# One woven section for the last two attention layers of a four-layer kernel

## The reference

```python
# second layer here ("L2"): 16 heads, 16 wide
a = layer_norm(ctx) ; Q = x @ Wq.T ; K = a @ Wk.T ; V = a @ Wv.T
scores = where(mask, Q K' / 4, -inf) ; out = softmax(scores) V @ Wo.T
x = x + tanh(gate) * out
# third layer here ("L3"): 32 query heads, 8 key heads, 8 wide
q = x @ Wq + bq ; k = ctx @ Wk + bk ; v = ctx @ Wv + bv
scores = q k' / sqrt(8) + mask ; out = softmax(scores) v @ Wo + bo
x = layer_norm(out + x) * gamma + beta
```

## Time and profile before

| | |
|---|---|
| median of 3 runs | 1299.11 us (1297.94 to 1301.02) |
| profiled execution, its own time | 1306.43 us |
| its span, first to last instruction | 1304.7 us |
| the last two layers in it | from 946.1 us to the end |
| TensorE busy over the span | 1163.8 us (89%) |
| VectorE, ScalarE, GpSimd busy | 852.4, 638.6, 655.9 us |

### The profile page before, as it was taken

One profiled execution on the slowest core, in us unless ns is written; L12 is line 12 of the kernel. 1 busy time (PEld: TensorE's weight loads), 2 busy tenths in 40 slices (PEclk: granted clock), 3 DMA queues, 4 the chain that ended last, 5 costly groups with the idle time before them and its releaser, 6 DMA issues. The chain is left out here.

```text
span 1304.7 us, 20610 instructions
## 1 busy us (share of the span) xinstructions
PE 1163.8 (89%) x7388; PEld 903.4 (69%) x7388; DVE 852.4 (65%) x2097; ACT 638.6 (49%) x1428; POOL 655.9 (50%) x677
## 2 busy tenths in 40 slices
PE   6999999999999999999999769986768998899994
PEld 4788888888888888888788624433436765666664
DVE  6776665766756766667756555985545657666756
ACT  3655655556655565455662114203133672477770
POOL 3665665556646565466763032770022661277760
PEclk9999999999999999999999869998888999899997
DMA  6210121112210112012102000000020000000000
GB/s 205 66 49 17 66 65 49 48 35 65 66 49 21 62 65 66 23 43 65 65 18 80 17 0 1 1 0 1 0 90 1 2 2 1 1 1 2 2 2 33
DMA packets 35110, 47.05 MB, mean 36 GB/s; under 512 B 3865, under 2 KB 22082, under 8 KB 35010
## 3 DMA queue, kind: packets, MB, share of 16 engines
q1 hardware_dynamic: 34640, 44.83, 10.7%
q10 hardware_dynamic: 370, 0.91, 0.2%
HBM read 44.69 MB, written 1.05 MB: 35 GB/s over the span
## 5 line engine op out<-in xcount | busy, mean ns | idle before, releaser
L444 POOL TENSOR_TENSOR a_prob<-a_prob,a_inv_total 128x512 f32<-128x512 f32 x128 | 144.3, 1127 | 208.3 <-DVE a_inv_total L732 208.3
L1583 POOL TENSOR_TENSOR l_scores<-l_scores,l_neg_max 128x512 f32<-128x512 f32 x144 | 147.8, 1041 | 103.1 <-DVE l_neg_max L1573 102.8
L1573 DVE CUSTOM_DVE_ANT_0 l_scores<-psum,mask 128x256 f32<-128x256 f32 x384 | 139.8, 421 | 72.9 <-PE psum L1526 72.9
L637 ACT ACTIVATE a_prob<-psum,a_neg_max 128x257 f32<-128x257 f32 x256 | 119.2, 473 | 94.2 <-DVE a_neg_max L729 93.5
L1604 ACT ACTIVATE l_prob_T<-psum 128x512 f32<-128x512 f32 x192 | 108.8, 590 | 37.2 <-PE psum L1540 37.2
L1540 PE MATMUL psum<-ident,l_scores 128*128 128x128 f32 x768 | 117.8, 292 | 7.3 <-POOL l_scores L1583 4.3
L1540 PEld LDWEIGHTS psum<-ident,l_scores 128*128 128x128 f32 x768 | 86.3, 147 | 42.1 <-issue 19.8
L736 DVE TENSOR_TENSOR a_probT_lo<-psum,a_probT_hi 128x512 fp32r<-128x512 f32 x128 | 88.0, 688 | 32.7 <-ACT a_probT_hi L641 32.1
L566 PE MATMUL psum<-ident,a_prob 128*128 128x128 f32 x512 | 77.8, 274 | 24.1 <-DVE a_probT_lo L736 21.7
L566 PEld LDWEIGHTS psum<-ident,a_prob 128*128 128x128 f32 x512 | 60.0, 140 | 44.7 <-issue 21.2
L729 DVE TENSOR_REDUCE a_neg_max<-psum 128x2 f32<-128x514 f32 x128 | 87.3, 682 | 1.2 <-PE psum L486 1.2
(11 more groups left out here) (331 smaller groups left out, 3294.9 us busy)
## 6 DMA issues: line engine op xcount, KB each, us to landing
wk_raw<-in_L_xattn_wk SPq DMA_DIRECT2D x16, 512.0 KB, 6.4
wq_raw<-in_L_xattn_wq SPq DMA_DIRECT2D x16, 512.0 KB, 5.7
wv_raw<-in_L_xattn_wv SPq DMA_DIRECT2D x16, 512.0 KB, 3.9
wo_raw<-in_L_xattn_wo SPq DMA_DIRECT2D x16, 512.0 KB, 4.0
ctx_rows<-in_ctx SPq DMA_DIRECT2D x3, 512.0 KB, 4.6
x_rows<-in_x SPq DMA_DIRECT2D x2, 512.0 KB, 9.6
mask<-in_mask_Bx1xSxS_ff SPq DMA_DIRECT2D x1, 1024.0 KB, 9.0
out_dram<-fin_y SPq DMA_DIRECT2D x4, 256.0 KB, 2.1
```

Source lines behind the costliest of these rows:

```text
L444: pool.tensor_tensor(prob[:, m % 4, :, 0:S], prob[:, m % 4, :, 0:S], rtot[:, m % 4, :].unsqueeze(2).to_broadcast([P, 2, S]), ALU.mult)
L637: act.activation(prob[:, m % 4, q, 0:S + 1], s_bank(g)[:, q, 0:S + 1], ACT.Exp, bias=negm[:, m % 4, q:q + 1], accum_out=tot[:, m % 4, q:q ...
L1573: e = dve.tensor_tensor_reduce(sc[:, i % SC, q, :], s_bank(i)[:, q * S:(q + 1) * S], masks[:, b * NM + q % NM, :], 1.0, BIG, ALU.add, ALU. ...
L1583: pool.tensor_tensor(sc[:, i % SC, :, :], sc[:, i % SC, :, :], m[:, i % SC, :].unsqueeze(2).to_broadcast([P, 2, S]), ALU.subtract).then_in ...
```

## The change

The ten blocks become one. `last_layers_orders` writes one order per engine by hand: an opening, then all 192 heads in a row, then an ending. Everything else is cut into pieces, each of one bank: `XT2`, `CT`, `AT` (turns of `x`, context and normalised context), `Q`, `K`, `V` of one half of the sequences, `SQ`, `SK` (stacks), `OT`, `OB`, `OP` (turn and divide the sums, turn back, output product) of one sequence, and `XT3` (turn of the new `x`).

- The opening holds the first half's pieces of the second layer up to the stacks, in 8 banks. Then come the scores of heads 0 to 3, the first half's `V` and the second half's `AT`, and the heads.
- Behind head i's `turn`, TensorE does the piece `behind[i]`: one piece behind each of heads 0 to 25, 28 to 57 and 60 to 71, then one behind every second head from 73 to 95 and in 99 to 109, 131 to 141, 163 to 173, 179 and 181. All of them use bank 7, so a piece waits until the one before it is evicted. Sums have one bank (6) where they had two.
- VectorE takes the extremes up to head i + 2 before it evicts the piece behind head i. Projections are now read twice straight from their bank: ScalarE rounds (hi), then VectorE subtracts (lo).
- To GpSimd go: clearing and filling the selection matrices (40 small copies), scaling both query weights, negating the third layer's mask, ones and zeros beside the values, the third layer's output bias, and scale and offset of the final norm for sequences 0 to 2.
- Loads have a semaphore each. The third layer's mask lands in the context's rows once these are read.
- Moments and final norm are done sequence by sequence; only sequence 3's lie behind the last head.

The core of the diff:

```diff
-        with ExitStack() as st:
-            ln = LayerNorm(...)
-            run_layernorm(chip, ln, load, turns=((chip.x, xT), (chip.ctx, cT)), vector_then=make_mask, scalar_then=make_gate)
-        attend(L2, w2, xT, aT, (None, None, None), masks2, gated)
-        stage_turn_and_bias(chip, chip.x, xT, chip.rows[:, r:r + 1, :], mask3)
-        attend(L3, w3, xT, cT, (...), mask3, ...)
-        stage_final_norm(chip, out)
+    put(0, [('CT', 1, c) for c in range(NC)] + [('Q', 2, 1, c) for c in range(NC)] + [('K', 2, 1, c) for c in range(NC)]
+        + [('SQ', 2, 1, g) for g in range(4)] + [('SK', 2, 1, g) for g in range(8)] + [('V', 2, 1, n) for n in range(2)])
+    put(20, output_pieces(2, 0) + [('XT3', 0), ('K', 3, 0, 0)])
+    put(28, [('SK', 3, 0, g) for g in range(7)])
+    put(35, output_pieces(2, 1) + [('XT3', 1), ('SK', 3, 0, 7)] + [('Q', 3, 0, c) for c in range(NC)]
+        + [('SQ', 3, 0, g) for g in range(8)] + [('V', 3, 0, 0)])
...
+    put(163, output_pieces(3, 2), 2)
+    put(179, output_pieces(3, 3)[:2], 2)
+    ending = output_pieces(3, 3)[2:]
+    bank = {p: k % 8 for k, p in enumerate(opening)}
+    bank.update(zip(second, (7, 6, 4, 5)))
+    bank.update({p: F_BANK for p in behind.values()})
+    pe = [('F', p) for p in opening] + [('S', 0), ('S', 1)] + [('F', p) for p in second]
+    for i in range(HEADS):
+        pe.append(('T', i))
+        if i in behind:
+            pe.append(('F', behind[i]))
+        if i % 2 and i // 2 + 2 < HEADS // 2:
+            pe.append(('S', i // 2 + 2))
+        if i % 4 == 1 and i > 4:
+            pe.append(('A', i // 4 - 1))
...
+                def piece(p):
+                    kind, bank = p[0], ps[:, bank_of[p], :]
+                    if earlier[p]:
+                        landed(pe, [earlier[p]])
...
+                for i in range(HEADS):
+                    if not on_scalar(i):
+                        pool.wait_ge(s_read, i + 1)
+                        pool.tensor_tensor(sc[:, i % SC, :, :], sc[:, i % SC, :, :],
+                                           m[:, i % SC, :].unsqueeze(2).to_broadcast([P, 2, S]), ALU.subtract).then_inc(shifted, 1)
+                    extras(i)
+                inverse_deviation(B - 1)
```

More of the change, by code:

```diff
@@ L1305, in __init__ @@
         self.per_chunk = P // (4 * width)
-L2 = Small("l2", 16, 16, 16, 16 ** -0.5, 2)
-L3 = Small("l3", 32, 8, 8, 1.0 / float(np.sqrt(np.float32(8.0))), 1)
+        self.KC = max(1, self.kv_cols // P)
+        self.KR = min(P, self.kv_cols)
+SMALL = {2: Small(16, 16, 16, 16 ** -0.5, 2), 3: Small(32, 8, 8, 1.0 / float(np.sqrt(np.float32(8.0))), 1)}
 BIG = 3e38
-def stage_turn_and_bias(chip, rows, out, bias, mask):
-    nc, ps = chip.nc, chip.psum
[L1317 to L1337, removed]
@@ L1340, in stage_small_project @@
[L1340 to L1349, removed]
-    with ExitStack() as st:
[L1351 to L1358, removed]
-        with nc.Block() as block:
+N2, N3 = B * SMALL[2].H, B * SMALL[3].H
@@ L1379, in _ @@
[L1379 to L1388, removed]
@@ L1552, in sums @@
                                            pT[:, i % PT, t * S:(t + 1) * S], start=t == 0, stop=t == 1, tile_position=(0, 32 * j))
                     mm.then_inc(a_done, 1)
-                scores(0)
-                scores(1)
-                for i in range(N):
-                    turn(i)
-                    if i % 2 and i // 2 + 2 < N // 2:
-                        scores(i // 2 + 2)
-                    if i % 4 == 1 and i > 4:
-                        sums(i // 4 - 1)
-                sums(QUADS - 1)
@@ L1577, in _ @@
-            @block.gpsimd
-            def _(pool):
-                for i in range(N):
-                    if on_act(i):
-                        continue
-                    pool.wait_ge(s_read, i + 1)
-                    pool.tensor_tensor(sc[:, i % SC, :, :], sc[:, i % SC, :, :],
-                                       m[:, i % SC, :].unsqueeze(2).to_broadcast([P, 2, S]), ALU.subtract).then_inc(shifted, 1)
+                for kind, what in pe_order:
+                    if kind == 'F':
+                        if what == output_pieces(3, 3)[2]:
+                            pe.wait_ge(s_read, HEADS)
+                        piece(what)
+                    elif kind == 'S':
+                        scores(what)
+                    elif kind == 'T':
+                        turn(what)
+                    else:
+                        sums(what)
@@ L1597, in shift, with exp @@
                     e.then_inc(act_shifted, 1)
-                shift(2)
-                for i in range(N):
+                def exp(i):
                     act.wait_ge(turned, i + 1)
@@ new lines, in exp @@
+                    act.activation(pT[:, i % PT, :], t_bank(i), ACT.Exp, scale=1.0 if on_scalar(i) else -1.0).then_inc(exp_ok, 1)
+                for kind, what in act_order:
+                    if kind == 'E':
+                        evict(what)
+                    elif kind == 'exp':
+                        exp(what)
+                    elif kind == 'shift':
+                        shift(what)
+                    elif kind == 'keep':
+                        keep(what)
+                    else:
+                        act.wait_ge(ld['gate'], 16)
+                        act.activation(gate[:, :], gate[:, :], ACT.Tanh).then_inc(gate_ok, 1)
```

806 lines of the change are left out of this document (487 added, 319 removed).

## The result

The kernel after takes 1311.99 us (median of 4 runs, 1311.25 to 1314.12), the kernel before 1299.47 beside it (1297.94 to 1301.02). The ratio is 1.0099, 95% interval 1.0081 to 1.0116: slower. I had forecast 1278 and a range of 1256 to 1297.

The account below looks back on a forecast made before the run. TensorE was taken to bound the head loops: 192.3 us of heads, 71.3 of pieces and 31 of waits, with 27.4 of opening and 15.1 of ending. That was 21.4 less than 1299.1: 1277.7, say 1278 us, range 1256 to 1297.

Parts of the forecast that it names:

- TensorE's work moves and does not hide: Among the heads: pieces add their TensorE time, 71.3 us, to 192.3 of heads, 263.6 in all.
- Opening, head 0's turn 27.4 behind the start: Ahead of the heads: first scores after 21.4 us, against 51.3 before, and head 0's turn 6.0 later.
- Ending 15.1: Behind the last turn: the steps to the final store sum to 15.1 us, where 34.0 stood behind the sums.
- The third mask's transfer, the second sums bank, ScalarE's load at no cost: Among the heads: late mask transfer, sums bank and ScalarE's extra evictions cost nothing; ScalarE busy 104 of 141.
- term (a): Bank 7 among heads 0 to 71: TensorE waits for evictions, about 0.4 behind even-to-odd neighbours; 17 us, bounds 0 and 34.
- Term (b): GpSimd's added steps among the heads: 1.1 free per four third-layer heads; 5 us of waits, bounds 0 and 15.
- Term (d): VectorE's eviction, then extreme, shift and turn: about 2.8 against 3.0 of TensorE work; 2 us, bounds 0 and 10.
- Term (c): Third layer's loop: its wait of 0.30 stays where no piece stands, 15 groups of 32; 4.5 us.
- Term (e): TensorE's clock at the heads' start: half of one fall to 1.2 GHz charged; 2.5 us, bounds 0 and 7.
- Against the median: Whole kernel: the profiled execution lies 7 us above the median, and the difference carries over: 1299.1 - 21.4 = 1277.7.
- the heavy one: Among the heads: added GpSimd and VectorE work makes pieces behind odd heads wait too; 1294, up to 1306; chance 0.25.
- The slower one, by the clock: Heads 0 to 25: waits at bank 7 keep TensorE at 1.2 GHz; 41 us more, 1319; chance 0.07.

Follow-up runs that it names:

- shift_late: Kernel after with ScalarE's shift of head 4n+2 queued behind the eviction at head 4n, not ahead of it: 1296.66 us, ratio 0.9966 to before.
- one_reader: Kernel after with all stacks behind heads evicted by VectorE and none by ScalarE: 1301.86 us, ratio 1.0007 to before.
- old_shift: odd_dense with ScalarE's shift of head 4n+2 put back behind head 4n-1, as in the kernel after: 1278.79 us, ratio 0.9839 to before.
- free_slots: shift_late with VectorE's moments taken apart and all of GpSimd's extra steps behind heads 4n+2: 1288.57 us, ratio 0.9906 to before.
- spaced: Kernel after with pieces from head 52 on behind even heads only: 1309.11 us, ratio 1.0064 to before.
- offset_split: Kernel after with the final norm's scale and offset in four GpSimd steps of one tile, three heads apart: 1307.70 us, ratio 1.0052 to before.
- odd_dense: free_slots with pieces placed anew, every second, odd head from 59 to 129, and scores first behind heads 4n+1 up to 57: 1274.88 us, ratio 0.9795 to before.
- before_again: Kernel before, unchanged, for a second trace: one run of 1303.36 us, span 1301.6.
- loads_split: Kernel before with only the wait for thirteen transfers taken apart, mask and gate loaded first: 1289.86 us, ratio 0.9919 to before.

## Why the prediction was wrong, step by step

- *TensorE's work moves and does not hide:* right. It is TensorE that sets the end among the heads: 263.6 of work leave 53.6 of the 317.2 (52.8 when added up by instruction), where I had 31. TensorE is idle some 33 of them (the window rows above: 20.5 + 13.1, the last 0.8 behind the last turn), for 28.5 of waits in the forecast; the other 20 or so are no waits, and for these I had 2.5.
- *Opening, head 0's turn 27.4 behind the start:* 32.1. Both misses are the clock. The query products took 5.40 where I had put 3.5, behind 2.33 of waiting for GpSimd's scaling, and the value products 6.06 for 3.5. The other steps came close to what I had worked out: the mask's three steps on VectorE ahead of the stacks, the first extreme at 970.25 against "near 968".
- *Ending 15.1:* 15.3, right.
- *The third mask's transfer, the second sums bank, ScalarE's load at no cost:* the transfer landed in 5.6 us and nobody waited for it; the sums bank shows no wait. ScalarE's share is no higher than I took it to be. But I asked how busy ScalarE is, and not what stands ahead of what in its queue.
- *Waits, term (a), bank 7, 17 us:* **this is the step that failed.** Count and mechanism of the short waits are right: 31 pieces behind odd heads waited, and three more behind queries and keys, 0.97 to 1.13 (3.1 in all, 3.3 forecast). 22 of the 31 are 0.39 in the mean, as forecast. The other nine are 1.26 in the mean, 11.3 us where 3.9 were forecast: 23.0 in all for 17. "ScalarE's exponential is ahead of it in its queue and does not shorten that" was looked at; the shift ahead of both was not. shift_late took back 8.4 us of waits (with the clock 12.7 of over, and 1.3 per cent of the time); one_reader and old_shift confirm it from the other sides.
- *Term (b), GpSimd, 5:* the waits for its shift are 8.2 in the list of waits, and free_slots took back 8.2 of over with the moments. The small copies cost 0.18 each from one to the next, as hoped; what was wrong is the rule "1.1 is free per four heads", which is true only of one place in the four.
- *Term (d), VectorE's chain, 2:* it held for evictions, with one exception that I didn't cost, the 1.9 us of addition and moments together; its 1.04 for three times is part of the 8.2.
- *Term (c), third layer's slack:* 0.24 per group without a piece, for 0.30.
- *Term (e), clock, 2.5:* sums at half clock alone are 3.9 over, scores and turns come on top, and 4.4 more lie in the opening. Between 5 and 10 in all; shown by the rows at either level, not separated further. Some 4.5 of it, in heads 0 to 51, is not there in spaced and offset_split, though the waits are.
- *What I had no term for, the second step that failed:* the sum of 263.6 takes a piece at the time of its products among their like. Between heads it costs 0.1 to 0.2 more, most of all the stacks (a key stack of the second layer behind an odd head 0.43, for 0.23). Over the 100 pieces that is some 11 us by my estimate, more than the nine waits missed by. It is in odd_dense as well, whose 16.9 over hold 8.2 of idle time, so that at most 8.7 are left for it there. That it comes from TensorE's change between kinds of work is argued; no run takes it apart.
- *Against the median:* the profile shown was 7.3 above its median; I carried this over in full. The new profile of before, 3.1 shorter as a whole, is 4.7 shorter in the section that the change rebuilds; so most of the difference should have been dropped: up to 7 of the 34 us of the miss. The rest is 4.7 in the opening and 22.6 among the heads.

Of the rivals, the heavy one had a fitting price, 16 to 28 over the forecast where the heads came out 22.6 over, but that is luck: it let pieces behind even heads wait as well, or GpSimd and VectorE cost 18 more. In the trace no piece behind an even head waits more than 0.16, and the waits for GpSimd's shift are 8.2, for the 7 of terms (b) and (d). The slower one, by the clock over heads 0 to 25, gave a time near the one measured (1319) by another way: these heads stood at 0.95 and not at 0.50. The forecast's own test said it: a sum over 50 would prove it wrong, and it is 53.6, counted as the forecast's 31 were.

The Trainium skill, "TensorE: Matmul & The Clock Gate", Part 4, says that the full clock does not engage for transposes. The traces agree only in part: odd_dense has the same transposes among its heads, with products between them, and shows 1.00 over 119 and 162 us. In after the half clock among the first heads stands behind waits of about 1 us and more; in offset_split nearly the same waits leave the clock at 1.00: over heads 0 to 25 TensorE is idle 9.8 us of 65.0 in after, at a mean granted clock of 0.95, and 9.9 of 62.1 in offset_split, at 1.00.

What stays open: why heads 0 to 51 ran 4.5 us longer in the profile of after than in those of spaced and offset_split, with the same order and nearly the same waits; and what the first turn would need to come below 29.5 us.

## What to carry to other kernels

When pieces of work are woven into a loop, the cost of a piece is less its own engine's time than the order of every queue that reads it: for each read, list what is ahead of it in that queue and what each of these waits for, and put no step that waits for a third engine ahead of a read that the first engine waits for. Free time of an engine in a loop has a place: find between which two of its instructions the gap lies, and put the extra step there, whole. A piece between two others can cost more than among its like; time one in its place before a hundred are counted. A profile that lies above its median may carry waits and half clock of its own; ask in which stage they lie before they are carried over to a kernel that doesn't have this stage. And before a difference between two profiles is put down to an edit, compare the stretches that the edit leaves alone.

## What the runs showed that I had not expected

Waits of the same length had different prices. Waits that fell by 8.4 us brought 12.7 among the heads, since sums behind such a wait had taken 1.76 to 1.84 in after and not 1.00; but in spaced and offset_split sums behind waits as long took 1.00. So the 4.3 between the two is not a price of the waits that one can count on. And the wait for all transfers in the kernel before cost 10 us where the wait itself was 8.66: the query products behind it took 9.66 (8.77 in before_again), and 7.10 in loads_split, where the wait is gone.
